# A two-layer graph kernel: softmax shift split and first loads moved, a score buffer's break moved, an unrolled output projection

## The reference, cut to what matters

```python
h = relu(layernorm(x)); x = x + A_norm @ h @ W_in + A_norm.T @ h @ W_out   # adj is 3327 x 3327
h = relu(layernorm(x))
q, k, v = [(h @ W.T).reshape(128, n, 8) for W in (Wq, Wk, Wv)]             # 128 heads, 8 wide
a = softmax(einsum('dnh,dmh->dnm', q, k) * 128 ** -0.5 + 2 * adj, axis=2)
x = x + einsum('dnm,dmh->dnh', a, v).reshape(n, 1024) @ Wo.T
```

## Time and profile before

| what | value |
|---|---|
| profiled execution, its span | 10844.98 us, 10842.2 us |
| busy PE, ACT, DVE, POOL | 96%, 94%, 89%, 77% |
| first and last score matmul | 819.1 and 10722.7 us |
| one ACT sum (L1104), 3072 of them | 2395 ns mean |
| one ACT product (L1101), 4096 of them | 956 ns mean |
| granted TensorE clock, mean | 0.990 |

### The profile page before, as it was taken

One profiled execution on the slowest core, in us unless ns is written; L12 is line 12 of the kernel. 1 busy time (PEld: TensorE's weight loads), 2 busy tenths in 40 slices (PEclk: granted clock), 3 DMA queues, 4 the chain that ended last, 5 costly groups with the idle time before them and its releaser, 6 DMA issues. The chain is left out here.

```text
span 10842.2 us, 542229 instructions
## 1 busy us (share of the span) xinstructions
PE 10388.2 (96%) x216535; PEld 6735.1 (62%) x216535; DVE 9621.0 (89%) x10382; ACT 10161.1 (94%) x7714; POOL 8392.4 (77%) x4260
## 2 busy tenths in 40 slices
PE   7749999999999999999999999999999999999998
PEld 6616666666666666666666666666666666666666
DVE  7688999999998999999998999999998999999997
ACT  4359999999999999999999999999999999999996
POOL 4347888888887888888887888888887888888885
PEclk9889999999999999999999999999999999999999
DMA  6582111111112111111112111111112111111113
GB/s 228 173 270 61 42 42 42 42 42 42 42 42 82 42 43 42 42 42 42 42 42 81 43 42 42 42 42 42 42 42 81 42 42 42 42 42 42 42 42 85
DMA packets 579449, 652.51 MB, mean 60 GB/s; under 512 B 172173, under 2 KB 517907, under 8 KB 573523
## 3 DMA queue, kind: packets, MB, share of 16 engines
q1 hardware_dynamic: 576786, 621.07, 20.5%
q0 software_dynamic: 832, 1.71, 0.0%
HBM read 485.17 MB, written 137.18 MB: 57 GB/s over the span
## 5 line engine op out<-in xcount | busy, mean ns | idle before, releaser
L1084 DVE SCALAR_TENSOR_TENSOR at_sum<-attention_adj_t,at_score 128x832 f32<-128x832 f32 x9216 | 8805.5, 1017 | 961.2 <-PE at_score L1020 869.4
L1000 POOL TENSOR_TENSOR at_single<-at_single,attention_adj_t 128x832 f32<-128x832 f32 x4096 | 8056.1, 1989 | 1866.4 <-ACT at_single L1101 1827.6
L1020 PE MATMUL at_score<-at_q,at_k 128*32 128x512 bf16 (+1 forms) x106496 | 7213.9, 347 | 202.9 <-DVE at_sum L1084 148.0
L1104 ACT ACTIVATE at_sum<-at_sum 128x2496 f32<-128x2496 f32 x3072 | 7358.6, 2395 | 14.4 <-DVE at_sum L1084 14.3
L1020 PEld LDWEIGHTS at_score<-at_q,at_k 128*32 128x32 bf16 x106496 | 3572.7, 145 | 2368.9 <-DVE at_sum L1084 965.4
L1036 PE MATMUL at_acc<-at_sum,at_v 128*9 128x208 f32 x73728 | 4846.6, 339 | 3.4 <-issue 2.4
L1101 ACT ACTIVATE at_single<-at_score 128x832 f32<-128x832 f32 x4096 | 3718.3, 956 | 113.3 <-PE at_score L1020 112.9
L1036 PEld LDWEIGHTS at_acc<-at_sum,at_v 128*9 128x9 f32 x73728 | 1872.5, 91 | 906.7 <-issue 6.1
L1036 PE MATMUL at_acc<-at_single,at_v 128*9 128x208 f32 x32768 | 2155.4, 339 | 0.0
L1036 PEld LDWEIGHTS at_acc<-at_single,at_v 128*9 128x9 f32 x32768 | 833.0, 91 | 404.3 <-issue 1.5
L288 POOL TENSOR_TENSOR layer_col_acc<-layer_col_acc,st_a_rows 128x3328 f32<-128x3328 f32 x26 | 189.2, 7278 | 182.6 <-DMA st_a_rows<-in_adj_dram 182.6
(11 more groups left out here) (123 smaller groups left out, 1363.8 us busy)
## 6 DMA issues: line engine op xcount, KB each, us to landing
at_k<-k_parts_scratch SPq DMA_DIRECT2D x1536, 156.0 KB
at_q<-q_parts_scratch SPq DMA_DIRECT2D x4608, 13.0 KB
at_v<-v_scratch SPq DMA_DIRECT2D x512, 112.5 KB
adj_t_scratch<-st_a_t SPq DMA_DIRECT2D x26, 1664.0 KB, 7.6
st_a_rows<-in_adj_dram SPq DMA_DIRECT2D x25, 1663.5 KB, 9.2
attended_scratch<-at_o SPq DMA_DIRECT2D x1920, 7.3 KB
attention_adj_t<-adj_t_scratch SPq DMA_DIRECT2D x12, 2080.0 KB, 18.9
q_parts_scratch<-pr_partsq SPq DMA_DIRECT2D x39, 512.0 KB, 4.6
```

Source lines behind the costliest of these rows:

```text
L1000: pool.tensor_tensor(slot(n), slot(n), at[:, plan.chunk[n], :], ALU.mult).then_inc(multiplied, 1)
L1020: last = pe.matmul(score[plan.buffer(n)][32 * t:32 * (t + 1), a:b], keys[:, 32 * t:32 * (t + 1)], q[k][:, a:b], start=True, stop=True, til ...
L1084: dve.scalar_tensor_tensor(out=slot(n), in0=at[:, plan.chunk[n], :], scalar=2.0, in1=score[plan.buffer(n)][:, 0:NB], op0=ALU.mult, op1=ALU ...
L1104: act.activation(sums[buffer][:], sums[buffer][:], ACT.Exp).then_inc(exped, 1)
```

## The change

`split_shift` is no longer a block: its four DVE instructions stand in `bound_scores` ahead of the maximum, and SP stores each part when it is made, behind the loads of heads 0 and 1 and the adjacency prefetch, all in the block of the bound. The q, k and v tiles live outside `attend`, and are cleared in the bound's block by POOL and DVE. `attend` only loads the shift rows of the two heads. In the loop a head's shift load now comes after its v loads. The buffer's break is moved from the end of the body to step 27. The projection has a `raw` and a `result` tile per chunk, is unrolled, and SP does all its DMAs.

```diff
 def bound_scores(...):
         def _(sp):
             for dst, src, step, done in (...norms...): sp.dma_start(...)
+            sp.wait_ge(head_cleared, 6)
+            for k in range(2):
+                first_heads(sp, k, preloaded[k])
             for g in plan.prefetched:
                 load_group(sp, at_d, et_d, at, plan, g, 0, prefetched)
+            store_shift(sp, parts, shift_d, split, shift_stored)
...
             chain.done()
+            split_shift(dve, shift, parts, nk, split)
             dve.tensor_reduce(small[:, 1:2], shift[:, 0:N], AX_X, ALU.max).then_inc(top_ready, 1)
...
+    TURN = C + 1
     def buffer(self, n):
-        return n % self.n % SCORES
+        n %= self.n
+        return (n + (n >= self.TURN)) % SCORES
...
 def attend(...):
-                sp.wait_ge(cleared, CLEARED)
                 for k in range(2):
-                    load(0, k, k)
+                    sp.wait_ge(preloaded[k], LOADS - 16)
+                    sp.sem_inc(head_loaded[k], LOADS - 16)
+                    load_shift(sp, shift_d, 0, k, q[k], head_loaded[k])
...
 def project_out(...):
+        raw = [s.sb(f"raw{c}", [P, VW, P]) for c in range(C)]
+        result = [s.sb(f"result{c}", [P, F]) for c in range(C)]
+        unit = [c if c < 3 else 2 + c // 3 for c in range(C)]   # loads awaited one by one, then by threes
...
+            for c in range(C): ...sp.dma_start(raw[c]...).then_inc(loaded[unit[c]], 16)
+            for c in range(C):
+                sp.wait_ge(added, c + 1)
+                sp.dma_start(...out..., result[c][0:r, :]).then_inc(stored, 16)
...
+            invert(0)                # DVE
+            for c in range(C):
+                if c + 1 < C:
+                    invert(c + 1)
+                divide(c)
+                if c >= 2:
+                    add(c - 2)
```

More of the change, by code:

```diff
@@ L757, in _ @@
                     dve.wait_ge(kept, c + 1)
+                split_shift(dve, shift, parts, scores, split)
 def load_products(sp, qp_d, kp_d, q_at, q_n, q_sb, k_at, k_n, k_sb, done):
@@ L767, in load_products, with load_head, load_shift @@
             sp.dma_start(q_sb[at:at + H, 0:q_n], bass.AP(qp_d, a * H * TOK + q_at, [[TOK, H], [1, q_n]])).then_inc(done, 16)
[L770 to L796, removed]
+def load_head(sp, qp_d, kp_d, v_d, b, d, q, k_all, v, done):
+    load_products(sp, qp_d, kp_d, d * N + b * NB, NB, q, d * N, N, k_all, done)
+    sp.dma_start(v[:, 0:C - 1, :].rearrange("p j w -> p (j w)"),
+                 bass.AP(v_d, d * (N * VW), [[C * VW, P], [1, (C - 1) * VW]])).then_inc(done, 16)
+    for x, y in row_pieces(LAST):
+        sp.dma_start(v[x:y, C - 1, :], bass.AP(v_d, d * (N * VW) + (x * C + C - 1) * VW,
+                                               [[C * VW, y - x], [1, VW]])).then_inc(done, 16)
+def load_shift(sp, shift_d, b, d, q, done):
+    sp.dma_start(q[SHIFT_ROW:SHIFT_ROW + PARTS, :],
+                 bass.AP(shift_d, d * NP + b * NB, [[HEADS * NP, PARTS], [1, NB]])).then_inc(done, 16)
 class Steps:
@@ L914, in attend @@
         STORES = 16 * COLT
-        CLEARED = 8
         SCORE_LEAD = 12 if products else 8
@@ L1133, in project_out, with loads_of @@
+        loaded = [s.sem(f"loaded{u}") for u in range(unit[-1] + 1)]
+        cleared, stored = s.sem("cleared"), s.sem("stored")
+        inverted, divided, turned_ready, turned_kept, product, added = [
+            s.sem(n) for n in ("inverted", "divided", "turned_ready", "turned_kept", "product", "added")]
         block = ctx.enter_context(nc.Block())
         def rows_of(c):
-            return LAST if isinstance(c, int) and c == C - 1 else P
+            return LAST if c == C - 1 else P
+        def loads_of(c):
+            return [(0, P)] if rows_of(c) == P else row_pieces(LAST)
@@ L1154, in _ @@
+            sp.wait_ge(stored, 16 * C)
         @block.gpsimd
         def _(pool):
-            def store(c, k):
-                pool.wait_ge(added, c + 3)
-                r = rows_of(c)
-                pool.dma_start(bass.AP(out.tensor, c * (P * F), [[F, r], [1, F]]), result[k][0:r, :]).then_inc(stored, 16)
-                pool.wait_ge(stored, 16 * c + 16)
-                pool.sem_inc(result_free, 1)
-            pool.sem_inc(result_free, 2)
-            with pool.Fori(0, C // 2 - 1) as i:
-                for k in range(2):
-                    store(2 * i + k, k)
@@ L1186, in _ @@
[L1186 to L1196 removed]
+                    last = pe.matmul(py[c % 2][:, 0:F], turned[c % 2][:, h, :], keep["wo_t"][:, h, :], start=(h == 0), stop=(h == H - 1))
@@ L1215, in _, with invert @@
-            dve.sem_inc(added, 2)
-            for k in range(2):
-                dve.memset(raw[k][:], 1.0).then_inc(cleared, 1)
-            def divide(c, k, count):
-                dve.wait_ge(loaded[k], count)
-                dve.wait_ge(divided, c + 2)
-                dve.reciprocal(inv[:], raw[k][:, H, :]).then_inc(inverted, 1)
+            def invert(c):
+                dve.wait_ge(loaded[unit[c]], 16 * sum(len(loads_of(d)) for d in range(C) if unit[d] == unit[c]))
+                if c >= 2:
+                    dve.wait_ge(divided, c - 1)
+                dve.reciprocal(inv[c % 2][:], raw[c][:, H, :]).then_inc(inverted, 1)
@@ L1234, in _, with add @@
[L1234 to L1243 removed]
+            def add(c):
+                dve.wait_ge(product, c + 1)
+                dve.tensor_tensor(result[c][:], py[c % 2][:, 0:F], keep["x"][:, c, :], ALU.add).then_inc(added, 1)
```

188 lines of the change are left out of this document (89 added, 99 removed).

## The result

The kernel after took 10744.42 us (median of 4 runs, 10737.76 to 10747.32), the kernel before beside it 10843.29: a ratio of 0.9909, with a 95% interval of 0.9897 to 0.9921. It is faster by 99 us, forecast were 105. The profiled execution, 10737.76 us with a span of 10735.9, is shorter by 106.3 us than the one of before.

A forecast was written before the change was run, and what follows sets the result against it. ACT was taken to bound attention, which holds most of the time. 10844.98 less 76 (loop), 14 (front) and 15 (projection) gave 10740 us; own range 10715 to 10770, widened to 10694 to 10816.

The forecast's parts named there:

- The boundary (a): At the body's end in attention, step 0 no longer waits for step 102: 0.36 us back per body.
- The jump (b): At PE's loop jump, steps 11 to 12, PE comes further ahead: 0.37 us of the usual 0.65 wait goes.
- The new break (c): At step 27 PE waits for product 25's exponential and starts 0.32 us late; ACT's product 29 loses 0.11.
- Rival 4: Slower: step 27's wait is 0.54 us per body, the boundary gives nothing; 69 lost, 29 gained, 10885 us; chance 0.04.
- Sum of the loop: Attention's boundary, jump and new break together: 0.6 us per usual body over 127 boundaries, 76 us gained.
- Rival 1: Step 12's stall keeps its length however early PE is; 0.25 us per body, 32 us gained, 10784 us; chance 0.14.
- Rival 3: All the attention loop's loss goes, even the jump hidden: 127 us gained there, 10689 us; chance 0.06.
- Front: Softmax front, from the bound's block to attention's first scores: PE starts at 805 us, 14 us gained.
- Projection: Final projection with loads queued at once and no memsets: gain 14 to 16 us, taken as 15.

The follow-up runs named there:

- the run of that part alone: The kernel before with only the new place of the buffers' break: 10776.93 us, ratio 0.9939.
- the break at step 72: The kernel after with the buffers' break at step 72 (step 20 of the third head) in place of step 27: 10725.98 us, ratio 0.9896.
- the single breaks: The kernel after with buffers running up to step 36, down from 37 to 67, up again from 68, in place of one break: 10736.47 us, ratio 0.9900.
- the ends changed: The kernel after with the break at step 72, shift stores ahead of the prefetch, and projection chunks 0 to 5 awaited one by one: 10726.16 us, ratio 0.9888.

## Why the prediction was right

- **The boundary (a)**: forecast 0.36 back, measured 0.34; it is gone whole.
- **The jump (b)**: 0.37 of 0.65 forecast to go, 0.46 of 0.64 went. The mechanism held: PE came to step 11 further ahead, by 0.38 us, which is the forecast. Beyond it the stall itself was 0.11 shorter (steps 11 to 12 are 1.23 us apart in the mean, 1.34 before). The runs don't tell why. The prediction read the 1.41 us of the loop instruction as the jump's length; it is not PE's stall. Before, that record begins 0.36 us ahead of step 11's scores, in after 0.22 behind their start, so its median fell to 0.68 while the stall fell by 0.11. The sum did not use the 1.41.
- **The new break (c)**: 0.11 forecast, 0.24 measured. Mis-sized: product 25 lasts 0.99 us in the mean and not 0.88, so step 27 starts 0.42 late and not 0.32, and 0.19 of that is covered. Its start at step 12 is less late than before, and sets ACT's durations back less. The bodies without a jump in the run of two bodies per turn show the same: no loss at step 12, and 0.36 at product 29. Rival 4 named this mechanism, and was wrong that it would outweigh the rest.
- **Sum of the loop**: 0.34 + 0.46 - 0.24 = 0.56 per body against 0.6; mean undisturbed body 77.04 to 76.50, 0.55. 76 us forecast, 72.6 in the trace and 69.9 by the run of that part alone. That it is so near is in part luck: the shorter stall, which nothing forecast, made good most of what (c) cost too much.
- **Rival 1**, that no earlier arrival of PE helps at step 12, fell: the same jump, its stall up to 0.2 us apart, cost ACT 0.64, 0.18, 0.10 or 0.27 (before, after, the break at step 72, the single breaks). The cleanest pair is after and the single breaks: steps 11 to 12 are 1.23 and 1.22 us apart, but PE starts step 11 0.39 and 0.50 behind ACT's sum, and ACT loses 0.18 and 0.27. The cost to the bound is stall less lead. The Trainium skill (Runtime: NRT & Kernel Launch, Instruction fetch mechanics) says that a taken branch outside the fetched pages stalls the engine. The traces agree that a jump can stall PE and that the prefetch hint shortens it (steps 11 to 12 are 4.06 us apart without it); that what is waited for is a fetch, no row shows, and with the loop turned by two steps there is no stall.
- **Rival 3**, all the loss gone, did not come in any run: 1.0 us was read against starts of 76.0 per body, and by the estimate from the ends a body takes 76.27. By it only 0.77 of before's body was to be had.
- **Front**: 14 forecast, 13.8 measured. POOL's clearing took 7.34 (7.4), the head loads 11.1 (11.1). One load of the prefetch held SP for 3.4 us, and SP's first load in the attention came 53.4 us behind the block's first, not 52, but entry to first scores took 1.8 to 2.1 us and not 3: two misses that cancel.
- **Projection**: 15 forecast, 16.3. PE took up the third chunk 16.9 us behind the first load (17.0); the pace was 2.66 us per chunk and not 2.75, since no wait for DVE was left. Against it, from the end of the last product to the end of the kernel it took 5.2 us, where the sum had 2.6, or 4.8 with a drain.

Open: why the stall at a jump varies from 0 to 1 us from one body to the next and, at step 12, between kernels with the same loop code (0.10 lost at step 72's break alone, 0.19 with the ends changed); why it is nothing between steps 13 and 14; and what in ACT lengthens its instructions.

## What to carry to other kernels

A stall on an engine that feeds the bound costs the stall less that engine's lead: put unavoidable stalls far apart, and each where the lead is largest, not together. Read a bound's floor from the pace of its ends, not of its starts, before counting how much is left. And here the hint on the long loop was worth 526 us, while a body doubled to save jumps cost 57; turning the loop by two steps took the jump's stall away, but not the time, since ACT had no more to gain and the entry cost 6.4.

## What the hardware showed unexpectedly

ACT's products with starts 0.74 us apart lengthen from 0.86 to as much as 1.40 us as long as no start comes late. A late start sets them back, even where ACT's records leave no idle time between them: in after product 25 lasts 0.99 us, product 29, which starts 0.24 late, 0.87. A loop body of four heads jumps back with a branch of 0.68 us (median), the same body turned by two steps 0.36 and without a stall, one of eight heads 1.97, one of four without a hint 3.71. Per jump the last cost 4.1 us of time ((11270.06 - 10744.42) / 127), some 1.5 of it through the granted clock of 0.50 that followed most of the stalls.
